# The low part of h in the diagonal blocks: 64x64 quarters with turned copies, and other orders on the engines around them

## Chip, cores and metric

The kernel runs on one core of a Trainium2 chip. The metric is the time of one launch in device microseconds; the figure compared is the median of several runs. Engines are called TensorE (PE in the profile, PEld its weight loads), VectorE (DVE), ScalarE (ACT), GpSimd (POOL) and SyncE (SP, its DMA queue SPq).

## What is computed

Input x is 128 batches of 64 rows by 512 features, adj a 64x64 matrix of zeros and ones. The reference, cut:

```
W = adj * adj
x = layernorm(x + einsum('bnf,nm->bmf', x, W) + bias)          # call this h
z_l, z_g, v = h @ W_lang.T, h @ W_grav.T, h @ W_V.T
A_l = max(zn zn^T, 0) * not_eye        # zn = z_l / |z_l|
A_g = exp(-d2 / (2 sigma^2)) * not_eye # d2 from |z_g|^2 and z_g z_g^T
K = w_l * rows_normalised(A_l * adj) + (1 - w_l) * rows_normalised(A_g * adj)
out = layernorm(h + (K v) @ W_O.T)
```

Inputs and output are float32.

## The kernel before

The 128 batches are worked in 16 groups of 8 batches, 512 rows each. A group is handled in one `iteration`; iteration 0 and iterations 13 to 15 are written out, the twelve between stand in a loop of two. Iteration n projects group n, finishes group n-1 (`before`), prepares h of group n+1 (`nxt`), and scales and splits the inputs of groups n+2 (`split`) and n+3 (`third`). Each engine has its own instruction list in the order of the code, and semaphores hold the engines together.

Every float32 operand is split into a high and a low float16 part, and a product is three passes: high by high, high by low, low by high.

z z^T is not made by projecting h twice. For each side (lang, grav) the kernel has L, the lower block triangle of W^T W with its diagonal blocks halved in part (`half_of`), and makes P = L h^T in four blocks of 128 rows (`p_hi`, `p_lo`), from which `gram` makes h^T P, and `symmetrise` adds the transpose. `project(g, j)` makes block j % 4 of side j // 4 in the PSUM bank `unit_bank[j]`: one pass over the diagonal block for the low part of h (`l_hi` with `ht_lo`), then three full passes of 128x512 for every block below it, which is 10, 7, 4 and 1 passes for j % 4 = 0 to 3.

The diagonal block's products with the high part of h (`l_hi` and `l_lo` with `ht_hi`) are made in `diagonal_blocks(g, side)`: since the block is symmetric, three of its four 64x64 quarters do. Four quarters that use the four quadrants of the array are issued one behind another. A quarter whose operands lie in the wrong half of the partitions uses turned copies: `l_turn` of the weights, made once, and `ht_turn`, a copy of parts of `ht_hi` with the halves exchanged, made by two DMAs per group in `turn` on SyncE. Before it, `transposes` issues eight DMA transposes per group that make `ht_hi` and `ht_lo` from `h_hi` and `h_lo`.

Around that, in an iteration, TensorE runs: `mix(nxt, 0)`, `project` 0 to 3, the quarters of side 0, `mix(nxt, 1)`, `project` 4 to 7, `kernel_t(before)`, the quarters of side 1, `attend_gate` and `attend` for `before`, `values(g, 0)`, `gram`, `values` 1 to 3, `third_norm`, `spread`, `symmetrise`. ScalarE copies a projected block out as `p_hi`, VectorE subtracts it for `p_lo`. `ks_hi`, `ks_lo` and then `kt_hi`, `kt_lo` are the kernel matrix of `before`, plain and transposed by `kernel_t`; `attend_gate` waits for `kt_lo`, and `y` of the next group. `u_high`, `u_low` split the values. `add_bias`, `row_stats` (bn_stats), `row_moments`, `norm_rows` make h of the next group. On GpSimd stand `x_low`, `t_diagonal`, `h_low` for two of four parts and `inverse_norm`.

## Time and profile before

| | us |
|---|---|
| median of 3 runs | 575.25 |
| the runs | 574.25, 575.25, 577.51 |
| the profiled execution | 577.62 |
| its span | 575.8 |

| engine | busy us | share | instructions |
|---|---|---|---|
| PE | 551.4 | 96% | 6280 |
| PEld | 290.9 | 51% | 6280 |
| DVE | 466.9 | 81% | 1009 |
| ACT | 388.9 | 68% | 794 |
| POOL | 210.8 | 37% | 230 |

Matmuls are pipelined: a pass of 512 columns lasts 0.38 us in the profile, and the next one starts before it ends. What counts is the distance from start to start. The mean granted clock of TensorE is 0.991 of full speed, which is its upper level of 2.4 GHz nearly throughout. DMA engines are busy for 44.4% of the span. A row that ends with a bracket names the idle time ahead of it and what ended it.

### The profile page before, as it was taken

What the parts mean: (1) busy time and instruction counts of PE and PEld (TensorE: products, weight loads), DVE (VectorE), ACT (ScalarE), POOL (GpSimd) and SP (SyncE); (2) the same over time, 40 slices, a digit from 0 to 9 for tenths busy, and PEclk for the clock granted to TensorE, in tenths of its full rate; (3) what the DMA queues carried; (4) which work ended last, traced back from release to release, by engine and by line L of the source; (5) the groups of instructions that cost most, each with busy time, mean ns of one, the idle gap of its engine ahead of it and who ended that gap; (6) DMA issues with size and microseconds to landing.
All of it is one profiled execution on the core that took longest, in us unless ns stands there. A gap on an engine that the chain in (4) does not pass through costs nothing.

```text
span 575.8 us, 16176 instructions
## 1 busy us (share of the span) xinstructions
PE 551.4 (96%) x6280; PEld 290.9 (51%) x6280; DVE 466.9 (81%) x1009; ACT 388.9 (68%) x794; POOL 210.8 (37%) x230
## 2 busy tenths in 40 slices
PE   9989789999999999999999999999999999999893
PEld 6544544645454545546454545455464545454361
DVE  1676878798897979797988979797979989896645
ACT  2577736778687677777786876777767866636362
POOL 0132442625244252626152442526262534313021
PEclk9999899999999999999999999999999999999998
DMA  8764161565634435454535344354545332414103
GB/s 247 221 142 90 38 119 42 79 168 67 166 63 130 88 95 127 87 146 96 146 69 154 64 125 98 85 138 87 146 95 146 64 106 38 133 26 88 60 2 146
DMA packets 94845, 60.81 MB, mean 106 GB/s; under 512 B 73184, under 2 KB 75232, under 8 KB 94816
## 3 DMA queue, kind: packets, MB, share of 16 engines
q1 hardware_dynamic: 94816, 60.42, 44.4%
q8 instruction: 19, 0.31, 0.2%
q14 instruction: 10, 0.08, 0.0%
HBM read 21.27 MB, written 16.78 MB: 66 GB/s over the span
## 4 chain that ended last, share of the span: by engine, by line
PE 82%; SPq 6%; DVE 5%; DMA 4%; issue 1%; ACT 1%; POOL 0%; POOLq 0%; ACTq 0%; DVEq 0%
PE proj L538 21%; PE proj L497 18%; PE ps_t L552 8%; PE ps_k L538 7%; PE ps_k L497 6%; PE proj L508 4%; PE front L459 3%; PE ps_v L567 3%; PE ps_t L576 3%; PE ps_k L508 2%; SPq L361 2%; DMA o<-in_L_gnn_W_O 2%; PE ps_t L628 2%; PE front L628 2%; SPq L372 1%
## 5 line engine op out<-in xcount | busy, mean ns | idle before, releaser
L1433 POOL TENSOR_TENSOR x_lo<-x_in,x_hi 128x512 f16<-128x512 f32 x60 | 70.1, 1180 | 158.3 <-ACT x_hi L778 158.3
L538 PE MATMUL proj<-m_hi,ht_hi 128*64 128x512 f16 x384 | 73.8, 381 | 0.0
L538 PE MATMUL proj<-m_hi,ht_lo 128*64 128x512 f16 x384 | 73.4, 379 | 0.0
L538 PE MATMUL proj<-m_lo,ht_hi 128*64 128x512 f16 x384 | 73.4, 379 | 0.0
L1050 DVE TENSOR_TENSOR p_lo<-proj,p_hi 128x512 f16<-128x512 f32 x96 | 63.0, 683 | 9.1 <-ACT p_hi L788 8.0
L788 ACT ACTIVATE p_hi<-proj 128x512 f16<-128x512 f32 x96 | 53.4, 597 | 20.1 <-PE proj L508 20.1
L497 PE MATMUL proj<-ht_lo,l_lang_hi 128*128 128x512 f16 x144 | 54.7, 380 | 2.2 <-DMA ht_lo<-h_lo 1.7
L552 PE MATMUL ps_t<-ht_hi,p_hi 128*128 128x64 f16 x512 | 48.9, 196 | 3.8 <-DVE p_lo L1050 3.8
L1463 POOL TENSOR_TENSOR t_diag<-t_sb,eye 128x512 f32<-128x512 f32 x15 | 19.7, 1310 | 87.4 <-ACT t_sb L799 87.4
L782 ACT ACTIVATE h_hi<-h 128x512 f16<-128x512 f32 x64 | 39.5, 624 | 18.1 <-DVE h L1030 17.9
L552 PEld LDWEIGHTS ps_t<-ht_hi,p_hi 128*128 128x128 f16 x512 | 46.2, 100 | 10.5 <-issue 6.3
L1030 DVE TENSOR_SCALAR h<-y,mv,rstd 128x512 f32<-128x512 f32 x64 | 46.9, 739 | 4.3 <-POOL rstd L1421 1.4
L552 PE MATMUL ps_t<-ht_lo,p_hi 128*128 128x64 f16 x512 | 48.7, 196 | 0.0
L552 PE MATMUL ps_t<-ht_hi,p_lo 128*128 128x64 f16 x512 | 48.7, 196 | 0.0
L508 PE MATMUL proj<-ht_turn,l_turn 64*64 64x512 f16 x288 | 47.3, 380 | 0.0
L552 PEld LDWEIGHTS ps_t<-ht_lo,p_hi 128*128 128x128 f16 x512 | 46.3, 100 | 0.7 <-issue 0.7
L552 PEld LDWEIGHTS ps_t<-ht_hi,p_lo 128*128 128x128 f16 x512 | 46.3, 100 | 0.0
L834 ACT ACTIVATE o<-o,nmr,rstd 128x512 f32<-128x512 f32 x60 | 44.1, 803 | 1.2 <-DVE nmr L1132 0.8
L999 DVE SCALAR_TENSOR_TENSOR y<-front,xinv,bias_b 128x512 f32<-128x512 f32 x60 | 43.1, 739 | 0.2 <-PE front L459 0.2
L829 ACT ACTIVATE o_square<-o,omean 128x512 bf16<-128x512 f32 x60 | 42.5, 710 | 0.0
L1018 DVE BATCH_NORM_STATS2 stats<-y 128x6 f32<-128x512 f32 x64 | 42.1, 682 | 0.0
L772 ACT ACTIVATE x_in<-x_in,xscale 128x512 f32<-128x512 f32 x60 | 41.3, 714 | 0.0
(272 smaller groups left out, 1614.2 us busy)
## 6 DMA issues: line engine op xcount, KB each, us to landing
x_in<-in_x SPq DMA_DIRECT2D x32, 512.0 KB, 7.1
out<-o SPq DMA_DIRECT2D x15, 1024.0 KB, 5.1
ht_turn<-ht_hi SPq DMA_DIRECT2D x16, 192.0 KB, 2.6
ht_turn<-ht_hi SPq DMA_DIRECT2D x16, 128.0 KB, 2.4
w_raw_lang<-in_L_gnn_W_lang SPq DMA_DIRECT2D x4, 256.0 KB, 3.6
o<-in_L_gnn_W_O SPq DMA_DIRECT2D x1, 1024.0 KB, 10.8
w_raw_grav<-in_L_gnn_W_grav SPq DMA_DIRECT2D x4, 256.0 KB, 10.9
uv<-in_L_gnn_W_V SPq DMA_DIRECT2D x1, 1024.0 KB, 15.3
```

The source lines that it names most:

```text
L497: pe.matmul(unit_bank[j][:, :], a[s][:, blk(k, c), :], b[g.parity][:, k, :], start=(n == 0), stop=False, skip_group_check=True)
L508: return pe.matmul(unit_bank[4 * side + c][cols, :], w, x, start=False, stop=True, skip_group_check=True)
L538: mm = pe.matmul(value_bank[p][q * N:(q + 1) * N, :], a[g.parity][:, k, rows:rows + N], b[:, k, :], start=(n == 0), stop=(n == len(passes) ...
L552: mm = pe.matmul(ps_t[:, b * N:(b + 1) * N], a[:, c, b, :, :].rearrange("p s n -> p (s n)"), t[g.parity][:, c, b * N:(b + 1) * N], start=( ...
L788: act.activation(p_hi[:, j % 4, :, j // 4, :], by_batch(unit_bank[j]), ACT.Copy).then_inc(phi_ready, 1)
L829: act.activation(o_square[:, p, :], o[:, p, :], ACT.Square, scale=D ** -0.5, bias=omean[:, p:p + 1], accum_out=ovar[:, p:p + 1]).then_inc( ...
L834: act.activation(o[:, p, :], o[:, p, :], ACT.Identity, scale=rstd2[:, p:p + 1], bias=nmr2[:, p:p + 1]).then_inc(out_ready, 1)
L999: dve.scalar_tensor_tensor(out=y[:, MIXED[p], :], in0=front[p % 2][:, :], scalar=xinv[g.parity][:, 0:1], in1=bias_b[:, :], op0=ALU.mult, o ...
L1018: dve.bn_stats(stats1[:, MIXED[p], :], y[:, MIXED[p], :]).then_inc(stats1_ready, 1)
L1030: dve.tensor_scalar(h[g.parity][:, p, :], y[:, p, :], mv1[:, p, 0:1], rstd1[:, p:p + 1], ALU.subtract, ALU.mult).then_inc(h_ready, 1)
L1050: dve.tensor_tensor(p_lo[:, j % 4, :, j // 4, :], by_batch(unit_bank[j]), p_hi[:, j % 4, :, j // 4, :], ALU.subtract).then_inc(plo_ready, 1)
L1433: pool.tensor_tensor(x_lo[:, p, :], x_in[g.parity][:, p, :], x_hi[:, p, :], ALU.subtract).then_inc(xlo_ready, 1)
```

## The change

`diagonal_blocks` now makes three products in quarters: high by high, low weights by high h, and high weights by low h. For the third it needs `ht_turn` of `ht_lo` too, so the tile doubles and `turn` issues four DMAs per group, the last two behind a wait for all of `ht_lo`. `project(g, j)` loses its pass over the diagonal block: 9, 6 and 3 passes are left for j % 4 = 0 to 2, none for 3 and 7, which are not called any more; the bank of block 3 is opened by its first quarters. The waits that stood ahead of `project(g, 3)` stand ahead of the last pass of `project(g, 2)`, and wait for four turned copies.

```
@@ sync
             def turn(g):
-                sp.wait_ge(ht_hi_loaded[g.parity], g.half * 64 + 64)
                 if g is not groups[0]:
                     sp.wait_ge(proj_done, g.prev().count(12, 8))
-                sp.dma_start(ht_turn[L, 0:2, :], ht_hi[g.parity][GR, 0:3:2, :]).then_inc(ht_turned, 16)
-                sp.dma_start(ht_turn[GR, :, :], ht_hi[g.parity][L, 1:4, :]).then_inc(ht_turned, 16)
+                for part, (part_t, loaded) in enumerate(((ht_hi, ht_hi_loaded), (ht_lo, ht_lo_loaded))):
+                    sp.wait_ge(loaded[g.parity], g.half * 64 + 64)
+                    sp.dma_start(ht_turn[L, part, 0:2, :], part_t[g.parity][GR, 0:3:2, :]).then_inc(ht_turned, 16)
+                    sp.dma_start(ht_turn[GR, part, :, :], part_t[g.parity][L, 1:4, :]).then_inc(ht_turned, 16)
@@ tensor, project
-                passes = [(c, l_hi, ht_lo)] + [(k, a, b) for k in range(c + 1, DC)
-                                               for a, b in ((l_hi, ht_hi), (l_hi, ht_lo), (l_lo, ht_hi))]
-                if j == 3:
-                    pe.wait_ge(ht_turned, g.count(32, 32))
...
+                passes = [(k, a, b) for k in range(c + 1, DC)
+                          for a, b in ((l_hi, ht_hi), (l_hi, ht_lo), (l_lo, ht_hi))]
                 for n, (k, a, b) in enumerate(passes):
+                    if n == len(passes) - 1 and j == 2:
+                        pe.wait_ge(ht_turned, g.count(64, 64))
...
+                    if n == len(passes) - 1 and j == 6:
+                        pe.wait_ge(plo_ready, g.count(8, 3))
@@ tensor, diagonal_blocks
+                products = ((0, 0), (1, 0), (0, 1))
...
-                for part in range(2):
-                    quarter(3, L, L, part)
-                    quarter(3, GR, GR, part, turned=2)
-                    quarter(2, GR, L, part, turned=1)
-                    mm = quarter(2, L, GR, part)
+                for n, (w, x) in enumerate(products):
+                    quarter(3, L, L, w, x, start=(n == 0))
+                    quarter(3, GR, GR, w, x, turned=2)
+                    quarter(2, GR, L, w, x, turned=1)
+                    mm = quarter(2, L, GR, w, x)
                 mm.then_inc(proj_done, 2)
@@ tensor, iteration
                 project(g, 1, first)
-                project(g, 2, first)
                 if first:
                     pe.wait_ge(xsum_ready, 2)
                     pe.wait_ge(xbase_ready, 1)
                     x_norm(split, x_norm_start)
-                project(g, 3, first, mixed=nxt)
+                project(g, 2, first, mixed=nxt)
...
                 project(g, 6, first)
-                project(g, 7, first)
@@ scalar, iteration
                 p_high(g, 4, first)
-                p_high(g, 5, first)
                 if has_square:
                     x_squares(third, 0)
+                p_high(g, 5, first)
```

The other engines get other orders. On ScalarE `x_high(split, 0)`, `ks_high`, `x_high(split, 1)` and `x_high(split, 2)` change places with their neighbours among the `p_high`, `u_high(g, 0)` goes from behind `h_high(nxt, 0)` to behind `h_high(nxt, 3)`, `u_high(g, 3)` ahead of `rectify`, and `normalise(before, 0)` ahead of `exponent`. On VectorE `u_low(before, 3)` comes first, `rows_low` goes behind `p_low(g, 2)` and one `add_bias`, `kt_low` ahead of the last `row_stats`, `residual(before, 0)` ahead of `p_low(g, 5)`, `u_low(g, 0)` behind `diagonals`, and `u_low(g, 1)` and `u_low(g, 2)` ahead of `shifted` and `out_shift`. On GpSimd `x_low(split, 2)` goes from the end of the iteration to ahead of the statistics of `nxt`.

TensorE, iteration 0: the end of the full passes of side 0 and the first quarters. `proj0` to `proj2` and `ps_t` are the banks of blocks 0 to 3. Before:

```order
L497 MATMUL proj2<-ht_hi0,l_lang_lo 128x512
L465 MATMUL ps_v<-xsum,ones16 128x1
L497 MATMUL ps_t<-ht_lo0,l_lang_hi 128x512
L508 MATMUL proj0<-ht_hi0,l_lang_hi 64x512
L508 MATMUL proj1<-ht_hi0,l_lang_hi 64x512
L508 MATMUL proj1<-ht_turn,l_turn 64x512
L508 MATMUL proj0<-ht_turn,l_turn 64x512
L508 MATMUL proj0<-ht_hi0,l_lang_lo 64x512
L508 MATMUL proj1<-ht_hi0,l_lang_lo 64x512
L508 MATMUL proj1<-ht_turn,l_turn 64x512
L508 MATMUL proj0<-ht_turn,l_turn 64x512 x2
```

After:

```order
L501 MATMUL proj2<-ht_hi0,l_lang_lo 128x512
L513 MATMUL proj0<-ht_hi0,l_lang_hi 64x512
L513 MATMUL proj1<-ht_hi0,l_lang_hi 64x512
L513 MATMUL proj1<-ht_turn,l_turn 64x512
L513 MATMUL proj0<-ht_turn,l_turn 64x512
L513 MATMUL proj0<-ht_hi0,l_lang_lo 64x512
L513 MATMUL proj1<-ht_hi0,l_lang_lo 64x512
L513 MATMUL proj1<-ht_turn,l_turn 64x512
L513 MATMUL proj0<-ht_turn,l_turn 64x512
L513 MATMUL proj0<-ht_lo0,l_lang_hi 64x512
L513 MATMUL proj1<-ht_lo0,l_lang_hi 64x512
L513 MATMUL proj1<-ht_turn,l_turn 64x512
```

The single full pass into `ps_t` is gone, and a third set of four quarters, with `ht_lo0`, follows the first two.

VectorE, the middle of a later iteration, from the scaled kernel matrix `ks_sb` to the first `p_lo` of side 1 (which reads `ps_k`). Before:

```order
L1110 TENSOR_TENSOR ks_sb<-a_sb,cfac 128x512
L1050 TENSOR_TENSOR p_lo<-proj,p_hi 128x8x64 x2
L1114 TENSOR_TENSOR ks_lo<-ks_sb,ks_hi 128x512
L1050 TENSOR_TENSOR p_lo<-proj,p_hi 128x8x64
L999 SCALAR_TENSOR_TENSOR y<-front,xinv,bias_b 128x512 x2
L1050 TENSOR_TENSOR p_lo<-ps_t,p_hi 128x8x64
L1018 BN_STATS stats<-y 128x6 x2
L1251 TENSOR_SCALAR hold<-stats 128x1
L1045 TENSOR_TENSOR kt_lo<-ps_v,kt_hi 128x256
L1023 BN_AGGR mv<-stats 128x2 x4
L1050 TENSOR_TENSOR p_lo<-ps_k,p_hi 128x8x64
L1050 TENSOR_TENSOR p_lo<-proj,p_hi 128x8x64
```

After:

```order
L1110 TENSOR_TENSOR ks_sb<-a_sb,cfac 128x512
L1050 TENSOR_TENSOR p_lo<-proj,p_hi 128x8x64 x3
L999 SCALAR_TENSOR_TENSOR y<-front,xinv,bias_b 128x512
L1114 TENSOR_TENSOR ks_lo<-ks_sb,ks_hi 128x512
L1018 BN_STATS stats<-y 128x6
L1050 TENSOR_TENSOR p_lo<-ps_t,p_hi 128x8x64
L999 SCALAR_TENSOR_TENSOR y<-front,xinv,bias_b 128x512
L1045 TENSOR_TENSOR kt_lo<-ps_v,kt_hi 128x256
L1018 BN_STATS stats<-y 128x6
L1256 TENSOR_SCALAR hold<-stats 128x1
L1023 BN_AGGR mv<-stats 128x2 x4
L1050 TENSOR_TENSOR p_lo<-ps_k,p_hi 128x8x64
```

`kt_lo` stands one BN_STATS and `hold` earlier, `ks_lo` one `p_lo` and one `y` later, and the residual `o,osum` two rows behind comes ahead of the next `p_lo`.

ScalarE, iteration 0, from the copy of the last block of side 0 to the first `h_hi`. Before:

```order
L788 ACTIVATE p_hi<-ps_t 128x8x64
L772 ACTIVATE x_in<-x_in,xscale 128x512 x4
L788 ACTIVATE p_hi<-ps_k 128x8x64
L788 ACTIVATE p_hi<-proj 128x8x64
L767 ACTIVATE x_square,xssq<-x_in 128x512
L788 ACTIVATE p_hi<-proj 128x8x64 x2
L778 ACTIVATE x_hi<-x_in 128x512 x4
L767 ACTIVATE x_square,xssq<-x_in 128x512 x2
L782 ACTIVATE h_hi<-h 128x512 x2
```

After:

```order
L791 ACTIVATE p_hi<-ps_t 128x8x64
L775 ACTIVATE x_in<-x_in,xscale 128x512 x4
L791 ACTIVATE p_hi<-ps_k 128x8x64
L770 ACTIVATE x_square,xssq<-x_in 128x512
L791 ACTIVATE p_hi<-proj 128x8x64 x3
L781 ACTIVATE x_hi<-x_in 128x512 x4
L770 ACTIVATE x_square,xssq<-x_in 128x512 x3
```

The three last `p_hi` now all stand behind `x_square`.

## Rows read from the trace of the kernel before

**Rows 1.** Waits of TensorE: engine, line, waited for, total us, times, longest us.

```profile
PE ps_t L552 <- DVE p_lo L1050: 3.8, 1, 3.8
PE ps_v L609 <- DVE kt_lo L1045: 2.0, 12, 0.2
```

**Rows 2.** Timeline, TensorE: start us, us, engine, line, operation, form, count.

```profile
368.62 0.39 PE L497 MATMUL proj<-ht_lo,l_lang_hi 128*128 128x512 f16 x1
...
373.17 0.38 PE L497 MATMUL ps_t<-ht_lo,l_lang_hi 128*128 128x512 f16 x1
373.47 0.40 PE L508 MATMUL proj<-ht_hi,l_lang_hi 64*64 64x512 f16 x2
...
400.38 0.39 PE L497 MATMUL proj<-ht_lo,l_lang_hi 128*128 128x512 f16 x1
```

**Rows 3.** Chain that ended last, 44 to 84 us: start us, us, what.

```profile
52.67 1.32 SPq L334
...
78.44 4.02 DMA ht_lo<-h_lo
...
82.69 1.47 PE proj L497 x6
```

**Rows 4.** Timeline, TensorE, the last block of quarters of side 0.

```profile
374.36 0.38 PE L508 MATMUL ps_t<-ht_hi,l_lang_hi 64*64 64x512 f16 x1
374.37 0.38 PE L508 MATMUL ps_t<-ht_turn,l_turn 64*64 64x512 f16 x1
...
374.58 0.38 PE L508 MATMUL ps_t<-ht_hi,l_lang_lo 64*64 64x512 f16 x1
```

**Rows 5.** Timeline, TensorE, around the gate of the same iteration.

```profile
380.39 0.32 PE L597 MATMUL ps_v<-eye,ks_hi 128*64 128x64 f16 x8
...
381.87 0.38 PE L508 MATMUL proj<-ht_hi,l_grav_lo 64*64 64x512 f16 x1
...
382.42 0.17 PE L609 MATMUL ps_v<-ones 128*128 128x1 bf16 x1 [0.16 <-DVE kt_lo L1045]
...
383.94 0.41 PE L538 MATMUL ps_k<-m_hi,ht_hi 128*64 128x512 f16 x2
```

**Rows 6.** VectorE: timeline there, and line L1114's ns (min/median/max).

```profile
380.41 1.27 DVE L1018 BATCH_NORM_STATS2 stats<-y 128x6 f32<-128x512 f32 x2
...
381.78 0.41 DVE L1045 TENSOR_TENSOR kt_lo<-ps_v,kt_hi 128x256 f16<-128x256 f32 x1
...
382.50 0.69 DVE L1050 TENSOR_TENSOR p_lo<-ps_k,p_hi 128x512 f16<-128x512 f32 x1
...
L1114 DVE TENSOR_TENSOR ks_lo<-ks_sb,ks_hi x15: 681/1231/1235, 90.8 to 534.6; 128x512 f16<-128x512 f32 x15
```

**Rows 7.** SyncE's queue: timeline, and DMA issues with KB, us to landing.

```profile
364.20 1.27 SPq L361 DMA_TRANSPOSE ht_lo<-h_lo  x1
...
366.22 0.60 SPq L380 DMA_DIRECT2D ht_turn<-ht_hi  x1
...
ht_turn<-ht_hi SPq DMA_DIRECT2D x16, 192.0 KB, 2.6
```

**Rows 8.** Timeline, ScalarE, iteration 0.

```profile
60.35 0.63 ACT L767 ACTIVATE x_square<-x_in 128x512 bf16<-128x512 f32 x1 [0.42 <-DMA x_in<-in_x]
...
60.98 1.06 ACT L788 ACTIVATE p_hi<-proj 128x512 f16<-128x512 f32 x2
```

**Rows 9.** Timeline, GpSimd, VectorE and TensorE ahead of `spread`, iterations 0 and 10.

```profile
68.24 1.82 POOL L1463 TENSOR_TENSOR t_diag<-t_sb,eye 128x512 f32<-128x512 f32 x1 [1.84 <-ACT t_sb L799]
...
76.77 0.68 DVE L1069 TENSOR_TENSOR r_sb<-eye,rr 64x512 f32<-64x512 f32 x1 [0.22 <-POOL rr L1469]
...
390.34 1.28 POOL L1463 TENSOR_TENSOR t_diag<-t_sb,eye 128x512 f32<-128x512 f32 x1 [6.08 <-ACT t_sb L799]
...
395.81 0.69 DVE L1069 TENSOR_TENSOR r_sb<-eye,rr 64x512 f32<-64x512 f32 x1 [0.17 <-POOL rr L1469]
...
397.49 1.10 PE L567 MATMUL ps_v<-r_sb,w_spread 128*128 128x512 f32 x2
```

129 lines of the change are left out of this document (64 added, 65 removed).

## The prediction, made before the changed kernel was run

> **What bounds the kernel now.** I read the busy table first: TensorE is busy for 551.4 of 575.8 us at a granted clock of 0.991, so one engine has the span. Then the waits of TensorE [rows 1]: one of 3.8 us before the first `gram`, and twelve, 2.0 us together, in front of `attend_gate` (L609) for `kt_lo`. Outside the first and the last iteration there is nothing else. Then the timeline: the first pass of `project` stands at 368.62 in one iteration and at 400.38 in the next [rows 2], a period of 31.76 us in which TensorE's only stop is the gate's. So in iterations 1 to 13 a column less on TensorE is time gained, as far as the engines that feed it keep up. The start is another matter. The chain of work that ended last runs there through SyncE's queue (L334 at 52.67, a load of `x_in`) and the landing of `ht_lo` (4.02 us), and only then reaches the first pass of iteration 1 at 82.69 [rows 3]. What the change does to the start must be counted by itself.
>
> **Part 1, TensorE's passes.** The 21 full passes from 368.62 to 373.17 start 0.216 us apart [rows 2]. Four quarters with four different quarter positions go out together: four start at 374.36 and 374.37, two of them shown, and the next four from 374.58 on, 0.22 us later [rows 4]. The change removes four full passes per side, 4 x 0.215 = 0.86 us, and adds twelve quarters, three slots, 0.65 us. That leaves 0.215 us per side and 0.43 us per group. The switch from full passes to quarters (373.17 to 373.47, 0.30 instead of 0.215 [rows 2]) happens as often as before.
>
> A rule speaks against this part. [rows 4] show `ps_t` written at the same moment by a quarter that contracts over the lower rows (from `ht_hi`) and one over the upper rows (from `ht_turn`), at full pace. The Trainium skill (TensorEngine Tiling (Array Packing), Gotcha 1: PSUM Pressure) states that different row tiles cannot access the same PSUM bank simultaneously. By that rule the last block of quarters would take two slots per product, three products would cost four slots per side instead of three, and the saving of part 1 would be nil; by the trace it is 0.43 us.
>
> **Part 2, the gate.** The last slot of quarters starts at 381.87; with the 0.30 us of a switch the gate could go at 382.17. It goes at 382.42 [rows 5], so its wait costs 0.25 us, not only the 0.16 us shown. It waits for `kt_lo`, 381.78 plus 0.41 us [rows 6]. Two things move it. On VectorE one `bn_stats` (0.64 us, half of 1.27) leaves the place in front of `kt_lo` [rows 6], and `hold` with it; `u_low(3)`, both `add_bias` and the rest only change places. So `kt_lo` can start at 381.78 - 0.64 = 381.14 and end at 381.55. `ks_lo` may shrink too: it takes 0.68 us at least and 1.23 in the middle [rows 6], and in the new order it falls between two `x_lo` of GpSimd; I count nothing for that. On TensorE `kernel_t`, at 380.39 [rows 5], gets five passes ahead (one slot on the first side, four passes on the second, 1.08 us), hence 379.3, so `kt_hi` is out of the way by 380.2. The gate's own time is 382.17 - 0.43 = 381.74. That is later than 381.55: the wait goes. `kernel_t` in turn needs `ks_lo`, which now stands behind the third `p_lo` and one `add_bias`, some 1.3 us of work more (two rows like the 0.69 of [rows 6]). The p_hi copies come 0.43 us sooner and close gaps of that size in front of it, so it would end near 378.9: 0.4 us to spare. What is next: `values(0)` at 383.94 [rows 5] would come at 383.26 and needs the fifth `p_lo`, at 382.50 [rows 6] now and at about 382.3 then, done at 383.0. 0.26 us to spare, the thinnest of all.
>
> **Part 3, the turned copies.** SyncE adds two DMAs per group. In the steady part the last `ht_lo` transpose is issued at 364.20; the second `ht_turn` DMA is issued at 366.22, for 0.60 us; the queue is then free at 366.8, and such a copy lands 2.6 us after issue [rows 7]. The transpose must land first. Taking 2.6 us for it as well, that is 366.8; the new DMAs go at 366.9 and 367.5 and land by 370.2. TensorE asks for them before the 18th pass, 368.62 + 17 x 0.215 = 372.3: 2.1 us to spare. Behind them on SyncE stand the store and the reload, which wait for ScalarE anyway. Cost nothing; if each landed 4.0 us after issue, as the slow `ht_lo` did [rows 3], still nothing.
>
> **Part 4, the start.** Here SyncE is on the path. Two more DMAs (0.60 us each and a gap [rows 7], 1.3 us) stand ahead of the weight turns and of the load at 52.67 [rows 3]. That load releases `x_square` at 60.35 [rows 8], which becomes 61.65. Behind `x_square` there were two `p_hi` (60.98 on), now there are three [rows 8], 0.5 us more. The last `p_lo`, `norm_rows`, the `h_lo` and the eight transposes follow in a row up to the `ht_lo` that TensorE waits for [rows 1, 3]. So iteration 1 starts 1.8 us later, and the 0.43 us of iteration 0 are lost in the wait for `p_lo`. Bounds: 0.5 us (the load lands when it did) and 2.8 us (SyncE also waits 1 us for the first `ht_lo`).
>
> **Part 5, the other moves.** `u_high(0)` goes behind `h_high(3)`, so `u_low(0)` delays `nsq`, which feeds `rr`, `r_sb` and then `spread`. Now `r_sb` is done at 396.5 and `spread` starts at 397.49 [rows 9]. GpSimd's row from `t_diag` on (390.34) sets `rr`, and moves with `gram`; `nsq` must be ready by then and just is. Margin 0.7 us or so, cost nothing. Its price if the cover goes is the second rival. Other moves, `u_high(3)` ahead of `rectify` and `x_low(2)` ahead of the statistics, fill idle time: nothing.
>
> **The sum.** Start +1.8. Twelve periods (iterations 1 to 12, those with the wait) at 0.43 + 0.25 = 0.68: -8.2. Iteration 13: -0.43. Iterations 14 and 15 have no `mix` to come and no gate wait; they give between nothing and 0.43 each, and I take 0.3, since TensorE is better supplied than not: -0.6. Together -7.4. The profiled execution took 577.62 us (span 575.8 and 1.8 around it), so it would take 570.2. It lies 2.4 us above the median of 575.25; against that median the forecast is 567.9 us.
>
> **Rivals.**
> A, the forecast: 565.5 to 569.5. Chance 0.62.
> B, VectorE takes the gain of the gate: the fifth `p_lo` or `kt_lo` comes 0.25 us or more later than I reckon, each period gives 0.43. For it: the margins of 0.26 us are thinner than my reading of gaps. Against: five rows move out of the way. 12 x 0.43 + 0.43 + 0.6 - 1.8 = 4.4, thus 570.9. With a start at its upper bound, 572. Chance 0.20.
> C, slower, the stretch before `spread`. From `t_diag` to the end of `r_sb` it takes 6.2 us in the steady part but 9.2 us in iteration 0, where VectorE and GpSimd stretch each other's rows (`t_diag` 1.82 instead of 1.28) [rows 9]. The new `t_diag` would start 0.68 us earlier, at 389.66, and `spread` could go at 396.8. Below 7.1 us nothing happens, above 7.8 us the period is longer than now. At 9.2 us `r_sb` is 2.05 us late, 1.4 us per period net, 12 x 1.4 + 1.8 - 1.0 = +17.6: 593. Chance 0.06.
> D, the change does not do what it says: the third product's quarters don't lie side by side in the last block. Then only the gate gives, 12 x 0.25 - 1.8 = 1.2: 574. [rows 4] speak against it. This is the result that the rule of the Trainium skill (TensorEngine Tiling (Array Packing), Gotcha 1: PSUM Pressure) would have. Chance 0.04.
> E, the start loses more than 2.8 us or the late copies delay `ht_turned` in the crowded start, and half the gain goes: 572 to 574. Chance 0.08.
>
> **Range and chances.** A and B hold 0.82. The lower end takes the start at 0.5 us, 0.43 for each of the last two, and 1 us for the spread of the runs: 565.5. The upper end is B with the dear start: 572.3. About 0.5%, 2.9 us, is what a measurement of this kernel can tell from none. Faster by more than that: A, B and a little of E, 0.83. Within it: D and the rest of E, 0.10. Slower: C and a share for what I don't see, 0.07.
>
> **What would show it.** In the changed profile: the period between first `project` passes at 31.1 us (B: 31.3); no wait at the gate; `kernel_t` about 10.7 us after the first pass instead of 11.8; no wait for `ht_turn` before the 18th pass; `x_square` of iteration 0 near 61.7 and iteration 1's first pass near 84.5 instead of 82.69. Wrong would be: a new idle row in front of `values`, `gram` or `spread`, or slots of quarters wider than 0.22 us.

## The result, and the profile after the change

The changed kernel takes 571.4 us, median of 5 runs (569.7 to 572.7), where the kernel before takes 575.8 in 5 runs beside it. The ratio is 0.991, 95% interval [0.988, 0.994], so 4.4 us are gained by the medians and 3.6 to 6.9 by the interval. The forecast was 567.9 us and the range 565.5 to 572.3. The direction was right and the time lies in the range, but 3.5 us above the forecast and outside rival A's own bracket, 565.5 to 569.5. The profiled execution took 572.66 us with a span of 570.9; that of before took 577.62 and 575.8. So 4.96 us are gained between the two, where the sum said 7.4.

First one period, TensorE's share of it by the window view: start and end, length, then busy us of TensorE's matmuls (count), of its weight loads, of VectorE, ScalarE and GpSimd, then granted clock and DMA. After the change:

```profile
365.10:396.20 31.10, 31.10 (x404) 16.39 (x401) 27.37 (x60) 24.16 (x50) 13.38 (x14) 1.00 0.52 124
```

And the same for the iteration of [rows 2] in the kernel before:

```profile
368.62:400.38 31.76, 31.60 (x388) 16.48 (x385) 27.86 (x60) 23.89 (x50) 13.35 (x15) 1.00 0.46 109
```

The period fell from 31.76 to 31.10 us, and TensorE is now busy in all of it. The timeline of TensorE in that period (start, length, engine, line, operation):

```profile
365.10 0.39 PE L501 MATMUL proj<-ht_hi,l_lang_hi 128*128 128x512 f16 x1
...
370.62 0.38 PE L513 MATMUL ps_t<-ht_hi,l_lang_lo 64*64 64x512 f16 x1
370.62 0.38 PE L513 MATMUL ps_t<-ht_turn,l_turn 64*64 64x512 f16 x1
...
370.84 0.38 PE L513 MATMUL ps_t<-ht_lo,l_lang_hi 64*64 64x512 f16 x1
370.84 0.38 PE L513 MATMUL ps_t<-ht_turn,l_turn 64*64 64x512 f16 x1
...
375.79 0.28 PE L602 MATMUL ps_v<-eye,ks_hi 128*64 128x64 f16 x6
...
378.23 0.18 PE L614 MATMUL ps_v<-ones 128*128 128x1 bf16 x1
...
379.76 0.41 PE L543 MATMUL ps_k<-m_hi,ht_hi 128*64 128x512 f16 x2
...
396.20 0.39 PE L501 MATMUL proj<-ht_hi,l_lang_hi 128*128 128x512 f16 x1
```

They answer to [rows 2, 4, 5]. `kernel_t` starts 10.69 us after the first pass (11.77 before), the gate 13.13 (13.80 before) and shows no wait. The third product's quarters start 0.22 us behind the second's. VectorE there, to compare with [rows 6] (the first row, the second `add_bias`, is needed below):

```profile
367.75 0.75 DVE L999 SCALAR_TENSOR_TENSOR y<-front,xinv,bias_b 128x512 f32<-128x512 f32 x1
...
374.33 0.68 DVE L1114 TENSOR_TENSOR ks_lo<-ks_sb,ks_hi 128x512 f16<-128x512 f32 x1
...
376.78 0.42 DVE L1045 TENSOR_TENSOR kt_lo<-ps_v,kt_hi 128x256 f16<-128x256 f32 x1
...
378.33 0.69 DVE L1050 TENSOR_TENSOR p_lo<-ps_k,p_hi 128x512 f16<-128x512 f32 x1
```

`kt_lo` is done 1.0 us before the gate instead of after it. Then the places that TensorE waits at in the whole execution, the view of the waits (us in total, times, longest), against [rows 1]:

```profile
PE ps_t L557 <- DVE p_lo L1050: 5.5, 1, 5.5
...
PE proj L501 <- DMA ht_lo<-h_lo: 1.7, 2, 1.1
PE proj L501 <- issue: 1.3, 1, 1.3
...
PE ps_v L572 <- issue: 0.5, 1, 0.5
PE proj L501 <- DMA ht_turn<-ht_lo: 0.2, 1, 0.2
```

The twelve gate waits are gone. In their place stand the wait of `gram` in iteration 0, 1.7 us longer than before, and a handful in front of iterations 1, 2, 14 and 15. I write Tn for the start of iteration n's first pass. The differences Tn+1 - Tn, read from TensorE's timeline:

| | before | after | change | predicted |
|---|---|---|---|---|
| start of the span to T1 | 82.69 | 84.16 | +1.47 | +1.8 |
| iteration 1 | 31.83 | 31.84 | +0.01 | -0.68 |
| iteration 2 | 31.75 | 31.37 | -0.38 | -0.68 |
| iterations 3 to 12 | 317.63 | 311.04 | -6.59 | -6.8 |
| iteration 13 | 31.64 | 31.08 | -0.56 | -0.43 |
| iteration 14 | 31.26 | 32.67 | +1.41 | -0.3 |
| T15 to the end | 49.0 | 48.7 | -0.3 | -0.3 |
| sum (span) | 575.8 | 570.9 | -4.9 | -7.4 |

Ten iterations in the middle behave as forecast. The 2.5 us that are missing went in iteration 14 (1.7) and in iterations 1 and 2 (1.0); the rest of the rows cancels. In iterations 1 and 2 the waits can be named from the timelines. The first pass of iteration 2 waits 0.54 us for `ht_lo`, and the 18th pass, due 3.67 us after the first, starts at 3.81 in iteration 1 and at 3.94 in iteration 2, where the last `ht_turn` lands only at 3.82.

The first row needs a second look. It holds the setup ahead of T0, whose code is the same, and which took 45.26 us before and 44.87 after. From T0 to T1 the change is 39.29 - 37.43 = +1.86 us. The 0.39 us between the setups are not the change's. In the profiled execution of before, TensorE waits 1.05 us there for the load of W_O, which landed 10.77 us after its issue; in that of the changed kernel it landed after 8.78 us, without a wait. The experiments ask three things: are the two parts really a sum; what sets the start; and what happens in iteration 14.

### The profile page after: what moved, and what is told of

It is laid out like the page before. It is cut to its first block, busy times and chain, and to the rows that moved or that the text cites. A ratio compares the mean times of both kernels' runs of the same rounds, so it can differ in the third digit from the quotient of the medians.

```text
span 570.9 us, 16726 instructions
## 1 busy us (share of the span) xinstructions
PE 544.7 (95%) x6536; PEld 289.8 (51%) x6536; DVE 461.1 (81%) x1009; ACT 392.6 (69%) x794; POOL 211.0 (37%) x230
## 4 chain that ended last, share of the span: by engine, by line
PE 81%; SPq 8%; DVE 5%; DMA 3%; issue 1%; ACT 1%; POOL 0%; POOLq 0%; ACTq 0%
PE proj L543 18%; PE proj L501 15%; PE ps_t L557 8%; PE ps_k L543 7%; PE proj L513 6%; PE ps_k L501 5%; SPq L361 5%; PE ps_k L513 4%; PE front L460 3%; PE ps_v L572 2%; PE ps_t L581 2%; PE ps_t L633 2%; PE front L633 2%; PE ps_t L513 2%; SPq L372 1%
## 5 line engine op out<-in xcount | busy, mean ns | idle before, releaser
L1050 DVE TENSOR_TENSOR p_lo<-proj,p_hi 128x512 f16<-128x512 f32 x96 | 60.6, 683 | 10.4 <-ACT p_hi L791 10.4
L513 PE MATMUL proj<-ht_turn,l_turn 64*64 64x512 f16 x432 | 68.1, 379 | 0.0
L791 ACT ACTIVATE p_hi<-proj 128x512 f16<-128x512 f32 x96 | 51.6, 594 | 21.0 <-PE proj L513 21.0
L1465 POOL TENSOR_TENSOR t_diag<-t_sb,eye 128x512 f32<-128x512 f32 x15 | 24.0, 1597 | 92.8 <-ACT t_sb L802 92.8
L1030 DVE TENSOR_SCALAR h<-y,mv,rstd 128x512 f32<-128x512 f32 x64 | 49.1, 773 | 2.8 <-POOL rstd L1423 1.4
L837 ACT ACTIVATE o<-o,nmr,rstd 128x512 f32<-128x512 f32 x60 | 45.6, 806 | 1.2 <-DVE nmr L1132 0.8
L999 DVE SCALAR_TENSOR_TENSOR y<-front,xinv,bias_b 128x512 f32<-128x512 f32 x60 | 44.5, 743 | 0.6 <-PE front L460 0.2
L1018 DVE BATCH_NORM_STATS2 stats<-y 128x6 f32<-128x512 f32 x64 | 43.7, 687 | 0.1
L775 ACT ACTIVATE x_in<-x_in,xscale 128x512 f32<-128x512 f32 x60 | 42.8, 719 | 0.0
L770 ACT ACTIVATE x_square<-x_in 128x512 bf16<-128x512 f32 x60 | 37.3, 632 | 6.3 <-DMA x_in<-in_x 4.5
```

The source lines that it names most:

```text
L513: return pe.matmul(unit_bank[4 * side + c][cols, :], w, x, start=start, stop=True, skip_group_check=True)
L775: act.activation(x_in[g.parity][:, p, :], x_in[g.parity][:, p, :], ACT.Copy, scale=xscale[g.parity][:, 0:1]).then_inc(xscaled_ready, 1)
L791: act.activation(p_hi[:, j % 4, :, j // 4, :], by_batch(unit_bank[j]), ACT.Copy).then_inc(phi_ready, 1)
L837: act.activation(o[:, p, :], o[:, p, :], ACT.Identity, scale=rstd2[:, p:p + 1], bias=nmr2[:, p:p + 1]).then_inc(out_ready, 1)
L999: dve.scalar_tensor_tensor(out=y[:, MIXED[p], :], in0=front[p % 2][:, :], scalar=xinv[g.parity][:, 0:1], in1=bias_b[:, :], op0=ALU.mult, o ...
L1018: dve.bn_stats(stats1[:, MIXED[p], :], y[:, MIXED[p], :]).then_inc(stats1_ready, 1)
```

## Experiments: are the two parts a sum?

**quarters_only** has TensorE and SyncE as changed and the other three engines as before.

> TensorE and SyncE as changed (third product as quarters, turned copies of ht_lo), the orders of VectorE, ScalarE and GpSimd as before. Theory 1, the two parts need each other: kt_lo keeps its place behind two bn_stats on VectorE, so TensorE reaches the gate 0.43 us sooner and waits there for most of that; period 31.5 to 31.76 us, idle time at the gate 0.2 us in the rows before and 0.4 to 0.6 now, total with the dearer start 574 to 577. Theory 2, the terms add up as I summed them: period 31.33 us, the wait at the gate as long as before, total some 571.5 (12 x 0.43 + 0.43 + 0.6 - 1.8 = 4.4 under the kernel before). In both the wait for ht_turn before the 18th pass is absent and x_square of iteration 0 starts near 61.9.

Measured: 575.83 us, ratio 1.000 [0.998, 1.002]. The period is 31.72 us: of the 0.43 us of part 1, 0.04 are left. Period and total are those of theory 1, but its place is wrong: the wait at the gate did not grow to 0.4 to 0.6 us, it stayed at 0.16. TensorE's and VectorE's timeline, period from 336.11:

```profile
340.19 0.39 PE L501 MATMUL proj<-ht_hi,l_lang_lo 128*128 128x512 f16 x1 [0.23 <-DVE y L1002]
...
349.88 0.17 PE L614 MATMUL ps_v<-ones 128*128 128x1 bf16 x1 [0.16 <-DVE kt_lo L1048]
```

```profile
339.39 0.74 DVE L1002 SCALAR_TENSOR_TENSOR y<-front,xinv,bias_b 128x512 f32<-128x512 f32 x1
...
347.87 1.27 DVE L1021 BATCH_NORM_STATS2 stats<-y 128x6 f32<-128x512 f32 x2
...
349.25 0.41 DVE L1048 TENSOR_TENSOR kt_lo<-ps_v,kt_hi 128x256 f16<-128x256 f32 x1
```

There is a second wait, which the prediction did not have: for `y` (the second `add_bias`) ahead of the last full pass of the first side. Before, that wait stood in front of the 22nd pass, 21 x 0.216 = 4.54 us after the first. The change moves it in front of the 18th, which goes 3.66 us after the first. `y` ends 4.02 us after it (339.39 + 0.74 - 336.11). In VectorE's order of before that is some 0.4 us too late. In the changed kernel it ends at 367.75 + 0.75 - 365.10 = 3.40: there `add_bias` stands ahead of the sum `deg`, a move that the list of the other engines' orders leaves out, and that gives it 0.6 us. The row before both, `a_sb`, waits for `e_sb` and starts 0.04 us ahead of the first pass in either kernel, so it is this swap and not ScalarE that brings `y` forward.

**quarters_kt** adds only one move of the reordering to it:

```
 row_stats(nxt, 2)
+kt_low(before)
 row_stats(nxt, 3)
 hold
-kt_low(before)
```

> TensorE and SyncE as changed, and of all the reordering only one move: kt_lo on VectorE ahead of the last bn_stats and of hold. In quarters_only the period was 31.72 us and TensorE stood at two places: at the gate for kt_lo (0.16 us shown) and in front of the 18th pass for y (0.21 to 0.23 us shown, add_bias of the third y rows ends there). Theory 1, these are two separate terms and kt_lo's place is only one of them: the wait at the gate goes, the wait for y stays, period 31.4 to 31.5, total 571.5 to 573. Theory 2, kt_lo's place is the whole of the reordering's worth: period 31.10 to 31.2, total 569 to 570. Theory 3, the wait merely moves, period stays at 31.7, total as before.

Measured: 574.27 us, ratio 0.998 [0.995, 1.000]; period 31.50 us. The gate shows no wait, and this one stays in every period:

```profile
339.94 0.39 PE L501 MATMUL proj<-ht_hi,l_lang_lo 128*128 128x512 f16 x1 [0.23 <-DVE y L1002]
```

Theory 1 holds for the period; the total came 1.3 us above its bracket, by the start, which took 1.4 us longer than in quarters_only though iteration 0 is the same code in both (see below).

**orders_only** is the reverse: VectorE, ScalarE and GpSimd as changed, TensorE and SyncE as before.

> The orders of VectorE, ScalarE and GpSimd as changed, TensorE and SyncE as before. Theory 1 (my sum): only the wait at the gate goes, 0.25 us a period, 12 x 0.25 = 3.0 us; the start stays nearly as before (first pass of iteration 1 at 82.7 to 83.2); iteration 14 loses about 1 us if the new place of the second h_lo behind norm_rows is what costs it. Period 31.50, total 572.5 to 574. Theory 2, kt_lo is set by TensorE's kernel_t, which keeps its late place here: the wait at the gate stays, period 31.7, total within 1 us of the kernel before.

Measured: 574.78 us, ratio 0.998 [0.997, 0.999]; period 31.53, first pass of iteration 1 at 82.75, iteration 14 at 31.99 us against 31.26. Theory 1 holds, with the total 0.8 us above its bracket.

The five periods follow from three terms (0.43 of work, 0.40 and 0.23 of waits), with 31.10 as the period without any wait after the change and 31.53 (0.43 more) before it:

| kernel | TensorE's work | wait for `y` | wait at the gate | period |
|---|---|---|---|---|
| before | 31.53 | none | 0.23 | 31.76 |
| orders_only | 31.53 | none | none | 31.53 |
| quarters_only | 31.10 | 0.40 | 0.22 | 31.72 |
| quarters_kt | 31.10 | 0.40 | none | 31.50 |
| changed | 31.10 | none | none | 31.10 |

The waits of this table are differences of periods, so the sums are no test by themselves. The one check is that the gate's wait comes out twice, 0.23 and 0.22. The views show less, 0.16 us at the gate and 0.23 for `y`; by their own starts the 18th pass comes 4.08 us after the first instead of 3.67. So the work saved is 0.43 us, but alone it is worth 0.04: VectorE then sets the pace. What the reordering is worth depends on it as well: 0.23 us by itself, 0.62 behind the quarters.

## Experiments: what sets the start

Before the change the load of `x_in` went out at 52.67 and `x_square` at 60.35 [rows 3, 8]. After it, in the timelines of SyncE, ScalarE and TensorE:

```profile
38.25 0.60 SPq L380 DMA_DIRECT2D ht_turn<-ht_lo  x1
38.90 0.61 SPq L381 DMA_DIRECT2D ht_turn<-ht_lo  x1
...
51.80 3.03 SPq L372 DMA_DIRECT2D l_turn<-l_grav_lo  x3
54.87 1.33 SPq L334 DMA_DIRECT2D x_in<-in_x  x2
```

```profile
61.91 0.63 ACT L770 ACTIVATE x_square<-x_in 128x512 bf16<-128x512 f32 x1 [2.19 <-DMA x_in<-in_x]
...
62.53 1.55 ACT L791 ACTIVATE p_hi<-proj 128x512 f16<-128x512 f32 x3
```

```profile
65.18 0.21 PE L557 MATMUL ps_t<-ht_hi,p_hi 128*128 128x64 f16 x1 [5.46 <-DVE p_lo L1050]
...
84.16 0.39 PE L501 MATMUL proj<-ht_hi,l_lang_hi 128*128 128x512 f16 x1 [1.12 <-DMA ht_lo<-h_lo]
```

**square_late** takes the first `x_square` out of the way of the `p_hi`:

```
-if has_square:
+if has_square and not first:
     x_squares(third, 0)
 p_high(g, 5, first)
 p_high(g, 6, first)
 p_high(g, 7, first)
+if first:
+    x_squares(third, 0)
```

> The changed kernel with the first x_square of iteration 0 behind the last p_hi on ScalarE, so that the late load of x_in no longer stands ahead of three p_hi. Theory 1 (my term for the start): the load is what makes the start late; p_hi no longer waits for it, the last p_lo ends near 62.5 instead of 65.0, the wait of gram shrinks from 5.5 to about 3, iteration 1 starts 1.5 to 2.5 us earlier, near 82; total 1.5 to 2.5 us under the changed kernel. Theory 2, the eight transposes of iteration 0 follow another chain (m_lo on VectorE, or h_hi behind the x_squares): iteration 1 starts within 0.5 us of 84.2.

Measured: 568.13 us, ratio 0.987 [0.985, 0.989]: 3.2 us below the changed kernel by the medians, 2.5 by the ratios, the largest effect of one moved line here. The three `p_hi` follow at once, and `gram` waits 2.66 us:

```profile
58.51 1.57 ACT L791 ACTIVATE p_hi<-proj 128x512 f16<-128x512 f32 x3
60.22 0.63 ACT L770 ACTIVATE x_square<-x_in 128x512 bf16<-128x512 f32 x1
```

```profile
61.27 0.19 PE L557 MATMUL ps_t<-ht_hi,p_hi 128*128 128x64 f16 x1 [2.66 <-DVE p_lo L1052]
```

From T0 to T1 it is 36.57 us instead of 39.29 (before: 37.43). Theory 1 is right, with slightly more than its 2.5 us. (T1 itself, at 80.32, is another 1.1 us early by a shorter setup.)

**reload_early** does it from the other side, `reload(groups[1])` on SyncE ahead of the grav half of `turn_weights` instead of behind it.

> The changed kernel with the load of x_in for group 3 ahead of the turning of the grav weights on SyncE instead of behind it: it goes out 6 to 7 us earlier. Theory 1 (the load sets the first x_square and through it three p_hi): x_square starts right behind the fifth p_hi, near 59.7 instead of 61.9; the grav weights are turned 1.3 us later, and TensorE may wait up to 1.3 us for them before its second side's quarters; iteration 1 starts 0.8 to 2 us earlier than 84.2, total 1 to 2 us under the changed kernel. Theory 2, the wait for the turned weights takes the whole gain: iteration 1 starts at 84 or later, total within 0.5 us of the changed kernel.

Measured: 569.71 us, ratio 0.991 [0.987, 0.994]. `x_square` starts at 58.76 directly behind the fifth `p_hi`, no pass of TensorE waits for the turned weights, and T0 to T1 is 36.95 us. So the mechanism is theory 1's. In the totals it shows less well: the median is 1.7 us below the changed kernel's, but the ratio is no different from its 0.991, and the six runs spread over 5 us.

**all_start** has both of these and the move of the next section.

> both_back with the load of x_in ahead of the turning of the grav weights as in reload_early. Theory 1, each of the two start moves takes the load out of the way of p_hi, so the second adds nothing: iteration 1 starts 36.4 to 37.0 us after iteration 0, total within 0.5 us of both_back. Theory 2, the load also delays what comes behind p_hi (x_square, x_hi and h_hi on ScalarE), and the two add: iteration 1 starts 0.5 to 1 us earlier than in both_back, 35.6 to 36.1 us after iteration 0.

Measured: 568.13 us, ratio 0.987 [0.984, 0.990]; T0 to T1 36.68 us. The second move adds nothing, theory 1.

**Why the start differs between equal programs.** quarters_only and quarters_kt have the same iteration 0, and T0 to T1 is 37.79 us in one and 39.18 in the other, 1.39 more. In both a fetch of instructions falls into the turning of `l_grav_lo` on SyncE, whose three issues take 2.42 and 2.99 us (3.03 in the changed kernel above), and the load behind them goes 9.32 and 10.14 us after T0: 0.82 of the difference. Another fetch stretches one transpose issue to 1.85 us in the one and 2.43 in the other: 0.58. Together 1.40. In the changed kernel the same three issues put the load 10.00 us after T0, where it was 7.41 before. That is 2.6 us later, twice the 1.3 us of the two copies: the other 1.15 us is one issue of `l_turn` that took 1.75 us instead of 0.60, beside a fetch. `gram` starts 20.31 us after T0 instead of 17.77, 2.5 us later. The transposes behind it then gave 0.6 us back, since in the kernel before a fetch had made the last `ht_lo` late [rows 3], and the setup gave 0.4. So the agreement of part 4 (+1.47 measured, +1.8 said) is partly luck: in quarters_only the same two DMAs cost 0.36 us between T0 and T1, with the sixth `p_hi` still ahead of `x_square`.

## Experiments: iteration 14

The end of iteration 14 in the changed kernel, VectorE, SyncE and TensorE:

```profile
511.04 1.76 DVE L1035 TENSOR_TENSOR h_lo<-h,h_hi 128x512 f16<-128x512 f32 x1
512.72 1.38 DVE L1030 TENSOR_SCALAR h<-y,mv,rstd 128x512 f32<-128x512 f32 x1
```

```profile
510.59 1.86 SPq L361 DMA_TRANSPOSE ht_hi<-h_hi  x1
...
517.98 1.26 SPq L361 DMA_TRANSPOSE ht_lo<-h_lo  x1
```

```profile
518.63 0.67 PE L572 MATMUL ps_v<-r_sb,w_spread 128*128 128x512 f32 x1 [0.53 <-issue]
...
522.16 0.38 PE L501 MATMUL proj<-ht_hi,l_lang_hi 128*128 128x512 f16 x1 [1.35 <-issue]
```

Two suspects: the second `h_lo`, which the change puts behind `norm_rows` and there meets GpSimd's `t_diag` (it takes 1.76 us); and the last `ht_lo`, issued at 517.98 and landed only 4.1 us later.

**hlow_back** puts the `h_lo` back:

```
 residual(before, 2, False)
+h_low(nxt, 1)
 residual(before, 3, False)
 norm_rows(nxt, 2, before)
-h_low(nxt, 1)
 norm_rows(nxt, 3, before)
```

> The changed kernel with the second h_lo on VectorE ahead of the third norm_rows again, as before. Theory 1, in iteration 14 the h_lo meets GpSimd's t_diag in its new place, takes 1.76 us instead of 0.69 and pushes norm_rows, nsq and r_sb: without it h_lo takes 0.69 again, spread starts 0.5 us earlier against the first pass of iteration 14, and up to 0.9 us of the wait for ht_lo behind it goes; total 0.5 to 1.4 us under the changed kernel, periods of iterations 3 to 12 at 31.10 as they are. Theory 2, the 0.9 us belong to an instruction fetch among the transposes and not to the order: the row of iteration 15's first pass keeps a wait of 1 us or more, total within 0.5 us of the changed kernel.

Measured: 570.10 us, ratio 0.989 [0.987, 0.992]. Iteration 14 takes 32.14 us instead of 32.67, and the wait in front of `spread` is gone; the steady period stays at 31.10. (The rest of what it gains, 1.0 us between T0 and T1, is the load again, 9.35 us after T0 instead of 10.00, and a fetch that stretches a transpose issue by 0.4 us less.) The `h_lo` takes 0.68 us, but what follows it is now what GpSimd stretches:

```profile
507.14 0.68 DVE L1035 TENSOR_TENSOR h_lo<-h,h_hi 128x512 f16<-128x512 f32 x1
...
508.42 1.75 DVE L1030 TENSOR_SCALAR h<-y,mv,rstd 128x512 f32<-128x512 f32 x2
```

and the wait for the last transpose is still there:

```profile
519.24 0.38 PE L501 MATMUL proj<-ht_hi,l_lang_hi 128*128 128x512 f16 x1 [1.77 <-issue]
```

So theory 1 has 0.5 us of the loss, theory 2 the larger rest. The timelines split it further. `spread` starts 29.14 us after the first pass in the changed kernel and 28.17 in hlow_back. Of this 0.97 us, 0.37 is the wait of the 18th pass for `ht_turn`, which hlow_back does not have: beside the fetch at 489.53 the last two copies took 3.9 and 4.0 us to land in the changed kernel, instead of the 2.6 and 2.8 of the steady part (3.4 and 3.5 in hlow_back, just in time). The other 0.6 is the `h_lo`; reload_early, with the `h_lo` in its new place and no such wait, has 28.77. Part of the gain is lost again behind `spread`, since the last `ht_lo` lands late in both: from `spread` to the next first pass it is 3.53 and 3.98 us. **both_back** joins this move and that of square_late.

> The changed kernel with both moves: the second h_lo ahead of norm_rows as before, and in iteration 0 the first x_square behind the last p_hi. Theory 1, the gains add, since they lie in different iterations (the x_square in iteration 0, the h_lo in iterations 0, 1, 2 and 14): 1.0 to 1.5 us under the better of the two, 566.5 to 567.5 us where the kernel before stands at 576. Iteration 14 lasts about 32.1 us as in hlow_back. Theory 2, they share a bound in the start (the row of transposes of SyncE): total within 0.5 us of square_late.

Measured: 568.66 us, ratio 0.988 [0.985, 0.991], 0.5 us above square_late instead of 1 below. By the trace the gains do add: from T0 to the end it is 520.8 us, against 522.2 in square_late and 526.0 in the changed kernel. But the setup ahead of T0, which is the same in all of them, took 46.50 us in this profiled execution and 43.75 in that of square_late. The reason stands in the trace: the load of W_O, issued at 5.84 in both, landed after 12.02 us here and after 8.83 there, and TensorE's first pass on it started at 17.91 and at 15.16, the same 2.75 us apart:

```profile
17.91 0.33 PE L738 MATMUL proj<-ident,o 128*128 128x128 f32 x1 [1.51 <-DMA o<-in_L_gnn_W_O]
```

Over the 14 profiled executions that landing takes 8.7 to 12.0 us. Where it takes over 11 us, T0 comes 34.5 us behind it; where it takes less than 10, TensorE doesn't wait for it, and T0 lies between 43.75 and 44.87. That spread is as large as the gains compared here, so profiled executions should be compared from T0 on.

What is left in iteration 14 is the last transpose. The DMA view of 516.3 to 520.1 (queue and kind with packets; then issues with us to landing; TensorE's first pass follows at 520.23):

```profile
q8 instruction: 1, 0.02, 1.9%
...
ht_lo<-h_lo SPq DMA_TRANSPOSE x1, 3.7
```

A fetch of instructions (16 KB) falls at 517.4, while the last `ht_lo` is under way. From iteration 13 on such fetches come once in some 250 recorded TensorE instructions; in iterations 3 to 12 there is none of that size. The Trainium skill (Runtime: NRT & Kernel Launch, Instruction fetch mechanics) states blocks of 16 KiB with 256 instructions and room for 2048 of TensorE's. The trace agrees with both: with the spacing, and in that the loop, two iterations of 805 matmuls and weight loads each, fetches nothing. The page calls the cost of crossing a block "mostly hidden"; in TensorE's own row it is (no wait stands beside the fetches of the changed kernel but the one for `ht_lo`), for the transposes here it is not.

**fetch_moved** tries to shift that fetch by lengthening TensorE's code in iteration 13, with `pe.wait_ge(wt_lo, 1)` twice before each of 36 passes.

> both_back, with two waits on a semaphore that has long been satisfied in front of each of the 36 full passes of iteration 13 on TensorE: no work is added or moved, only TensorE's code from there on is longer by 36 to 72 instructions, so that the fetches of 16 KB, which came once in 256 TensorE instructions on average, fall 1.4 to 2.7 us earlier in iteration 14. Theory 1, the wait of 1.5 to 1.8 us for the last ht_lo before iteration 15 comes from such a fetch (it stood 2.2 us ahead of iteration 15's first pass in the changed kernel, 7.8 us in the kernel before): the landing falls from 4.1 to 2.6 us, iteration 14 lasts 31.0 to 31.6 us instead of 32.1, total 0.5 to 1.2 us under both_back. Theory 2, the landing is slow there for another reason (the ht_turn copies behind it, or the loads): iteration 14 stays at 32.1 us. Iteration 13 may itself become up to 0.5 us longer by the waits.

Measured: 569.04 us, ratio 0.988 [0.985, 0.990]; iteration 14 31.92 us. The trace has 36 instructions more, and the fetch, at 516.0, moved only from 1.1 to 0.9 us behind the start of `spread` (515.08; the 0.4 us of the next expectation counts from the second of its two passes). It stood at the same place against the last `ht_lo`. The run doesn't decide.

**fetch_moved2** puts three such waits before each of 48 steps of `values`.

> both_back, with three satisfied waits in front of each of the 48 steps of values in iteration 13: 96 instructions more of TensorE's code from there on, no work added. In both_back the fetch came at 517.4, 1.1 us behind the start of spread and 2.8 us ahead of iteration 15's first pass; fetch_moved added 36 instructions, and it came at 516.0, 0.4 us behind the start of spread: still at the last ht_lo. TensorE goes through some 20 instructions a us in values, so 96 put the fetch 3 to 4 us ahead of spread. Theory 1, the fetch makes the last ht_lo late: it lands 2.5 to 2.7 us after its issue instead of 4.1, iteration 14 lasts 30.8 to 31.3 us instead of 32.07, total 0.8 to 1.2 us under both_back, less what the waits cost in iteration 13 (up to 0.5 us). Theory 2, the landing there is slow for another reason: iteration 14 stays at 31.9 to 32.1 us.

Measured: 567.46 us, ratio 0.985 [0.982, 0.988], the lowest median of all. The trace has 52 instructions more, not the 96 I had reckoned with, and the fetch comes at 512.91, 3.0 us ahead of `spread`. The last transpose, by the DMA view of 516.7 to 519.4, has no fetch beside it and lands in the usual time, 2.5 us instead of 3.7:

```profile
ht_lo<-h_lo SPq DMA_TRANSPOSE x1, 2.5
```

But iteration 14 is not shorter (32.35 us), because the fetch hit the sixth transpose instead, and SyncE's row waits behind it:

```profile
512.95 2.56 SPq L361 DMA_TRANSPOSE ht_lo<-h_lo  x1
515.55 1.26 SPq L361 DMA_TRANSPOSE ht_hi<-h_hi  x1
```

Half of theory 1 holds (what makes the landing late is the fetch), the time expected does not. **best** has the same code on top of all_start.

> all_start with the 96 instructions of fetch_moved2. Theory 1 of both: total 566.5 to 568 us where the kernel before stands at 576, 4 us under the changed kernel. By the second theory of fetch_moved2 it is that of all_start, plus 0.3 us for the waits.

Measured: 568.35 us, ratio 0.987 [0.984, 0.990]. Here the fetch (513.6) comes 0.7 us behind the sixth issue instead of with it, and costs the seventh 0.17 us:

```profile
512.89 1.26 SPq L361 DMA_TRANSPOSE ht_lo<-h_lo  x1
514.20 1.44 SPq L361 DMA_TRANSPOSE ht_hi<-h_hi  x1
515.69 1.26 SPq L361 DMA_TRANSPOSE ht_lo<-h_lo  x1
```

Iteration 14 is 30.45 us, 1.6 less than in both_back and 2.2 less than in the changed kernel, with no wait for `ht_lo` at all. A longer iteration 13 also gives the feeders more time, so it matters where the gain lies. `spread` starts 28.16 us after the first pass, as in both_back (28.18), and from there to the next first pass it takes 2.29 us instead of 3.89. So all of it is behind `spread`, where the fetch was. But the added instructions cost iteration 13 0.48 us, so the two iterations together are 1.0 to 1.1 us shorter than in all_start and both_back. Iteration 2 is 0.36 us longer than in all_start, and the total is no better than its. So the cause in iteration 14 is settled, but as a lever on the total this is worth nothing certain.

**The end.** T15 to the end has two lengths, in ten kernels with the same code there. It is 47.0 to 47.1 us in square_late, reload_early and both_back, and 48.6 to 48.8 in the changed kernel, hlow_back, fetch_moved, fetch_moved2, all_start, best and two_more. The window view of TensorE there (the clock stands behind the five engines), in the changed kernel and in both_back, each 5 us from 16.8 us after T15 on:

```profile
539.00:544.00 5.00, 5.00 (x58) 3.01 (x58) 1.41 (x6) 0.00 (x0) 0.00 (x0) 0.66 0.00 0
```

```profile
537.00:542.00 5.00, 4.92 (x102) 3.75 (x104) 1.47 (x6) 0.13 (x1) 0.00 (x0) 1.00 0.02 3
```

TensorE waits 2.78 us for `o` ahead of it in both. Then in the one the granted clock is at its lower level, 1.2 GHz, for 3.4 us (0.66 is the mean), and in the other it stays at 2.4 GHz: 1.65 us. With one profile of each I can't say what decides it. Of the kernels with other orders, that of before has the long end too (49.0 us), and quarters_only, orders_only and quarters_kt have not (47.4, 47.5 and 46.7), after waits of 2.5 to 2.8 us. So the profiled executions of before and after are alike in this, and those of before and of the three partial kernels are not; the periods are not touched. How many of the executions behind a median have the long end isn't known. The record does give each execution's mean granted clock: of 68 executions of the kernel before, 18 have 0.993 or more and a median of 574.5 us, the other 50 one of 576.7. The totals of square_late, both_back, all_start, fetch_moved2 and best, 567.5 to 568.7 us, can't be told apart; by their ratios all are 2 to 3 us below the changed kernel, with intervals that touch or overlap its own. square_late does it with one moved line, and it is the version I would keep.

**two_more** tests what the prediction counted at nothing, SyncE's added DMAs:

```
 sp.dma_start(ht_turn[GR, part, :, :], part_t[g.parity][L, 1:4, :]).then_inc(ht_turned, 16)
+sp.dma_start(ht_spare[L, part, :], part_t[g.parity][GR, 0, :]).then_inc(ht_turned, 16)
...
-pe.wait_ge(ht_turned, g.count(64, 64))
+pe.wait_ge(ht_turned, g.count(96, 96))
```

> The changed kernel with two more DMAs per group on SyncE: behind each pair of ht_turn copies one of 64 partitions from ht_hi or ht_lo into a spare tile, and TensorE waits for all six before its 18th pass. That doubles what the change itself added to SyncE. Theory 1 (my part 3: such copies cost nothing in the steady part): in the changed kernel the last ht_turn goes out 0.4 us ahead of the first pass and is wanted 3.66 us behind it; with two more it goes out 0.9 us behind it and lands near 3.4: period still 31.10 us. Where TensorE already waits for ht_turn (0.3 to 0.4 us in iterations 1 and 14) it waits up to 1.3 us longer, and the start loses up to 1.3 us through the load of x_in behind them: total 1.5 to 3.5 us above the changed kernel's 571.4. Theory 2, the copies collide with what else is moved (loads and stores): the period grows, by 0.3 us or more each, and the total is above 575.

Measured: 575.14 us, ratio 0.997 [0.994, 0.999]. The period is still 31.10 us, while the last copy now goes out 0.64 us behind the first pass (366.44; 1.09 in the iteration before) and lands at 2.9 or 3.4, where 3.67 is asked:

```profile
367.08 0.60 SPq L383 DMA_DIRECT2D ht_spare<-ht_lo  x1
```

That is theory 1. The total is 0.3 us above its bracket by the medians; it passes the 575 of theory 2, but the period, which theory 2 wanted longer, did not grow. The profiled executions are 2.4 us apart. The loss is all outside: iterations 2, 3 and 14 take 1.1, 0.3 and 0.8 us longer than in the changed kernel (iteration 1 0.4 less), and where the queue is full the wait stands in TensorE's row:

```profile
120.93 0.39 PE L503 MATMUL proj<-ht_hi,l_lang_lo 128*128 128x512 f16 x1 [1.24 <-DMA ht_spare<-ht_lo]
```

## Where the prediction was right and where it failed

**Part 1, 0.43 us per group: right**, and shown twice (31.53 to 31.10). Three products take three slots of 0.22 us, so rival D is refuted. So is, read as a cost in time and for this pattern, the rule of the Trainium skill that stood beside it (TensorEngine Tiling (Array Packing), Gotcha 1: PSUM Pressure): [rows 4] show two row halves writing `ps_t` at the same moment, the rows after the change show it for three products, with no slot lost.

**Part 2, the gate: right in size, incomplete in its reasons.** I gave 0.25 us; it is 0.23. `kernel_t` came at 10.69 us as worked out, `kt_lo` was done at 377.20, 12.10 us after the first pass (I had said 381.55 - 368.62 = 12.93, not counting what `ks_lo` gives back: 0.68 instead of 1.23). What I did not see is the wait for `y`: part 1 counted passes and slots, but not that the waits in front of unit 3 move 0.88 us ahead with it. I looked at one of them (`ht_turn`, 372.3) and not at `y`, which stands in the same place. It was harmless only since "both `add_bias` ... only change places" was not nothing: the second one ends 3.40 us after the first pass instead of 4.02, which is worth 0.40 us per period. The sum of 0.68 came out at 0.66 by a term I had left at nought on both sides. Rival B had the right mechanism, VectorE taking TensorE's gain, at the wrong row, and it decided only in quarters_only and quarters_kt.

**Part 3, SyncE: right in the steady part** and in two_more with twice the number. The last copy lands 2.3 us after the first pass, so 1.3 us were to spare, not 2.1. The "nothing" did not hold outside: the 18th pass comes 0.27 us late in iteration 2, where the copies stand behind a late `ht_lo`, and 0.37 in iteration 14, where `ht_lo` landed in time and the copies themselves took 3.9 and 4.0 us to land beside a fetch. The prediction had worked it out only for the steady part. Its bound, that landings of 4.0 us would still cost nothing, fails there, since the last copy went out at the first pass (0.01 us ahead of it) and not 1.1 us before it.

**Part 4, the start: the mechanism is right, the size partly luck.** square_late and reload_early show that the load of `x_in` is what the `p_hi` waited for. But the load went 2.6 us later after T0 and not 1.3, `gram` started 2.5 us later, and a quicker row of transposes and a shorter setup brought the sum back to +1.47. Its weight depends on the fetches, as said.

**Part 5 and rival C: right**; `r_sb` is at 391.98, later than it could be by a wait of 0.36 us for `rr`, and `spread` (393.31) starts without a wait. `u_low(0)` in front of `nsq` costs nothing there. In iteration 14 it is not so: `spread` waits 0.53 us, and hlow_back shows that it was the `h_lo` behind `norm_rows`.

**The sum: the term that failed is that of the edges.** "Iterations 14 and 15 ... I take 0.3" and "Twelve periods" took the last iteration and the first two for steady ones. Iteration 14 lost 1.41 us instead of gaining 0.3. Against best, which has none of the three, it is 2.22 us longer: 0.6 is the `h_lo`, 0.37 the wait for `ht_turn`, both ahead of `spread`, and the other 1.2 stands behind `spread`, where one instruction fetch falls on the last `ht_lo` (up to 1.6 between both_back and best). (The kernel before has a fetch in the same row of transposes too, where the issue at 519.22 took 2.27 us, but none at the last `ht_lo`.) Iterations 1 and 2 (1.0 us short) are the same kind, waits for `ht_lo` and `ht_turn`: hlow_back takes 0.4 us off the two, and in all_start they are 31.45 and 31.10 us, in best 31.46 and 31.47. How much of that is the order and how much the fetches, the runs don't separate.

The total of 571.4 us also lies where rival B stood (570.9, 572 with a dear start), but not for its reason: the periods are 31.10 us, as in A, and not 31.3. That the time is in the range is owed to a bracket that was there for another mechanism. That range also ends 0.4 us above what its terms give (570.9 + 1.0 = 571.9, against 572.3).
